# A feed-forward kernel on one core: the first butterfly of x moved from GpSimd into PSUM accumulation, early and late turns moved from DMA to TensorE, and all engine programs written out anew

## The reference

```python
w = weights[conditions]
y = jnp.einsum('bct,bcd->bdt', x, w)          # tokens (b, d), 512 features
h = hbitlinear(y, w_up, 8)                    # w_up (1024, 512)
h = jnp.square(jax.nn.relu(h))
out = x + hbitlinear(h, w_down, 8)            # w_down (512, 1024)

def hbitlinear(x, w, bits):
    xq = act_quant(fwht(x), bits)             # Walsh-Hadamard, then absmax quantization per token
    wq = weight_quant(w)                      # ternary, one scale: mean |w|
    return jnp.einsum('bsd,fd->bsf', xq, wq)
```

## Time and profile before

| what | us |
|---|---|
| median of 3 runs | 282.44 |
| lowest, highest run | 282.28, 285.0 |
| span of the profiled execution | 279.9 |
| what lies around the span (median less span) | 2.5 |
| PE busy | 246.1 (88%) |
| DVE busy | 204.7 (73%) |
| POOL busy | 181.4 (65%) |
| ACT busy | 147.4 (53%) |

### The profile page before, as it was taken

The page is one execution under the profiler, slowest core; times in us unless marked ns, Lnnn a source line. Parts: engine busy times, 40 slices in busy tenths (PEclk is TensorE's granted clock), DMA queues, the critical chain, the costliest instruction groups (busy, mean ns, idle before and its releaser), DMA issues.

```text
span 279.9 us, 6739 instructions
## 1 busy us (share of the span) xinstructions
PE 246.1 (88%) x2116; PEld 203.6 (73%) x2116; DVE 204.7 (73%) x341; ACT 147.4 (53%) x193; POOL 181.4 (65%) x231
## 2 busy tenths in 40 slices
PE   0266899799999999999999999999999899985872
PEld 0266797797979797979797888888888687754441
DVE  0145557799888697888878796969697977887632
ACT  2143588765647465655656565556462766641220
POOL 1333133869797979697979788887976467278510
PEclk9999999999999999999999999999999999998899
DMA  6865963245563745585664437434443325553364
GB/s 188 305 210 204 191 158 51 42 122 95 143 107 92 154 122 89 143 143 128 155 191 87 122 75 215 94 94 98 116 84 106 81 57 109 135 112 75 75 86 141
DMA packets 67369, 34.96 MB, mean 125 GB/s; under 512 B 57490, under 2 KB 57618, under 8 KB 67346
## 3 DMA queue, kind: packets, MB, share of 16 engines
q10 hardware_dynamic: 52432, 14.75, 28.4%
q1 hardware_dynamic: 14914, 19.93, 23.3%
HBM read 13.70 MB, written 8.39 MB: 79 GB/s over the span
## 4 chain that ended last, share of the span: by engine, by line
PE 61%; issue 9%; DMA 8%; POOL 6%; DVE 5%; ACTq 4%; ACT 3%; SPq 2%; POOLq 0%; DVEq 0%
PE u_ps L750 15%; PE h_ps L737 14%; PE o_ps L761 13%; PE y_ps L708 10%; PE z_ps L721 8%; DMA zqT<-zq 4%; POOL p L422 4%; ACTq L527 2%; DMA uqT<-uq 2%; ACT uq L547 2%; POOL u_deq L430 1%; DVE u_max L931 1%; ACTq L554 1%; DVE y L893 1%; DMA w_pair<-in_L_cond_weights_dram 1%
## 5 line engine op out<-in xcount | busy, mean ns | idle before, releaser
L422 POOL TENSOR_TENSOR p<-g 128x512 f32<-128x512 f32 x64 | 80.9, 1287 | 23.6 <-DVE g L924 22.9
L750 PEld LDWEIGHTS u_ps<-had_sb,p 128*128 128x128 f32 x512 | 61.0, 193 | 12.2 <-POOL p L422 7.1
L750 PE MATMUL u_ps<-had_sb,p 128*128 128x128 f32 x512 | 63.8, 278 | 6.8 <-POOL p L422 4.4
L737 PE MATMUL h_ps<-zqT,w_upT 128*128 128x256 f16 x512 | 61.8, 272 | 2.5 <-ACT g L534 1.3
L761 PE MATMUL o_ps<-w_downT,uqT 128*128 128x512 f16 x256 | 61.7, 384 | 2.4 <-DMA uqT<-uq 2.4
L385 POOL TENSOR_TENSOR x_half<-x_all 128x512 f32<-128x512 f32 (+1 forms) x32 | 40.9, 1300 | 25.9 <-PE y_ps L708 15.3
L737 PEld LDWEIGHTS h_ps<-zqT,w_upT 128*128 128x128 f16 x512 | 49.4, 98 | 9.5 <-issue 2.0
L547 ACT ACTIVATE uq<-u_ps,u_mul 128x1024 f16<-128x1024 f32 x32 | 35.6, 1114 | 34.2 <-DVE u_mul L944 28.2
L534 ACT ACTIVATE g<-h_ps 128x512 f32<-128x512 f32 x64 | 37.7, 595 | 21.8 <-PE h_ps L737 10.1
L931 DVE TENSOR_REDUCE u_max<-u_ps 128x1 f32<-128x1024 f32 x32 | 39.0, 1218 | 10.8 <-PE u_ps L750 10.7
L708 PE MATMUL y_ps<-w_pair,x_half 64*128 64x64 f32 x512 | 35.4, 293 | 12.1 <-DMA w_pair<-in_L_cond_weights_dram 12.1
(11 more groups left out here) (35 smaller groups left out, 142.1 us busy)
## 6 DMA issues: line engine op xcount, KB each, us to landing
x_all<-in_x_dram SPq DMA_DIRECT2D x32, 256.0 KB, 3.3
out_dram<-out_sb SPq DMA_DIRECT2D x32, 256.0 KB, 2.3
w_raw<-in_L_ffn_w_up_dram ACTq DMA_DIRECT2D x4, 512.0 KB, 4.4
w_raw<-in_L_ffn_w_down_dram SPq DMA_DIRECT2D x4, 512.0 KB, 4.9
w_pair<-in_L_cond_weights_dram SPq DMA_DIRECT2D x64, 16.0 KB, 2.2
zqT<-zq ACTq DMA_TRANSPOSE x32, 2.7
uqT<-uq ACTq DMA_TRANSPOSE x32, 3.1
had_sb<-in_hadamard_dram ACTq DMA_DIRECT2D x1, 64.0 KB, 3.6
```

Source lines behind the costliest of these rows:

```text
L422: nc.gpsimd.tensor_tensor(new[:, :, m, :], old[:, :, 0, :], old[:, :, 1, :], (ALU.add, ALU.subtract)[m]).then_inc(s_p8[k], 1)
L737: mm = nc.tensor.matmul(h_ps[u % 2][:, i, :], w_upT[:, q, f * P:(f + 1) * P], zqT[par][:, q, :], start=(q == 0), stop=(q == TC - 1))
L750: mm = nc.tensor.matmul(u_ps[:, c * P:(c + 1) * P], p8[par][:, c, k * P:(k + 1) * P], had_sb[:, :], start=True, stop=True)
```

## The change

`x_outer` is gone. `project` now streams for the first half of x's features the two copies (w, w), 128 columns, and for the second half (w, minus w), accumulated in the same PSUM place; ACT writes minus w once per tile (`negate_w`). Both kernels issue 16 matmuls per tile here. The two z halves of a tile are turned by one DMA, except tile 0, which PE turns (`first_turn`, with a copy by DVE). The last tile's u is turned by PE as well (`last_turn`, `last_copy`). The second half of tile 0's z goes into an h bank; the second halves of u in tiles 14 and 15 go into the h banks, and the second halves of their output into `z_ps`. Scale columns have a place per tile, so that the copies `keep_z` and `z_now` fall away. PE begins with 24 matmuls on constants (`warm`). x has 8 buffers of a tile instead of 16 tiles in place, w has 8 instead of 4, out_sb has two sets, zqT five. All five programs are written out call by call, without a loop, and in a new order.

```diff
-            def x_outer(t, half, par, h):
...
-                nc.gpsimd.tensor_tensor(x_half[h][:, :, :], xt[:, :, 0, :], xt[:, :, 1, :],
-                                        (ALU.add, ALU.subtract)[h]).then_inc(s_xh[h], 1)
+            def negate_w(t):
+                act.wait_ge(s_wc[t % NW], 16 * BT * (t // NW + 1))
+                nc.scalar.activation(ws[t % NW][:, :, 1, :], ws[t % NW][:, :, 0, :], ACT.Copy, scale=-1.0)\
+                    .then_inc(s_ws, 1)
...
-                                nc.tensor.matmul(y_ps[:, b, l, h, j, :],
-                                                 x_half[h][rows, j, l * P:(l + 1) * P], w[rows, j, :],
-                                                 start=True, stop=True)
+            for l in range(2):
+                for j in range(KP):
+                    for h in range(2):
+                        for b in range(2):
+                            w = ws[t % NW][rows, j, 0:1, :].broadcast_to([C, 2, C]) if h == 0 \
+                                else ws[t % NW][rows, j, :, :]
+                            mm = nc.tensor.matmul(y_ps[:, b, l, :, j, :],
+                                                  xs[t % NX][rows, j, h * 256 + l * P:h * 256 + (l + 1) * P], w,
+                                                  start=(h == 0), stop=(h == 1))
...
+            def warm():
+                for i in range(WARM):                              # WARM = 24
+                    nc.tensor.matmul(o_ps[:, 0:P], ones[:, :], ones[:, :], start=True, stop=True)
+            def first_turn(k):
+                for q in range(TC):
+                    mm = nc.tensor.transpose(zT_ps[:, (k * TC + q) * P:(k * TC + q + 1) * P],
+                                             zq[0][:, k, q * P:(q + 1) * P], ident[:, :])
+            def last_turn(k):
+                for m in range(FC):
+                    mm = nc.tensor.transpose(uT_ps[k][:, m * P:(m + 1) * P], uq[(TILES - 1) % 2][:, k, m * P:(m + 1) * P],
+                                             ident[:, :])
+        def own_home(t, k):
+            return k == 1 and t in LAST                            # tiles 14 and 15
+        def z_home(t, k):
+            return h_flat[:, T:2 * T] if (t, k) == (0, 1) else z_ps[:, :]
+        def u_home(t, k):
+            return h_flat if own_home(t, k) else u_ps[:, :]
+        def o_home(t, k):
+            return z_ps[:, :] if own_home(t, k) else o_ps[:, :]
...
+                act.dma_start(zqT[t % NZT][:, :, :, :].rearrange("p k q n -> p (k q) n"),
+                             zq[t % 2][:, :, :].rearrange("p k t -> p (k t)"), transpose=True)\
```

More of the change, by code:

```diff
@@ L196, in after @@
         def after(eng, semaphore, count):
[L198 to L231, removed]
+            if count > 0:
+                eng.wait_ge(semaphore, count)
@@ new lines, in _ @@
+            up(2, 3)
+            up(2, 2)
+            had_u(0, 1)
+            up(3, 1)
+            had_z(4, 1)
+            up(3, 0)
+            down(0, 0)
+            had_u(1, 0)
+            project(6)
+            had_z(5, 0)
+            up(3, 3)
+            up(3, 2)
+            down(0, 1)
+            had_u(1, 1)
+            up(4, 1)
+            had_z(5, 1)
+            up(4, 0)
+            project(7)
+            had_u(2, 0)
+            had_z(6, 0)
+            up(4, 3)
+            up(4, 2)
@@ new lines, in _ @@
+            down(1, 0)
+            had_u(2, 1)
+            up(5, 0)
+            had_z(6, 1)
+            down(1, 1)
+            had_u(3, 0)
+            up(5, 1)
+            project(8)
+            had_z(7, 0)
+            up(5, 2)
+            up(5, 3)
+            down(2, 0)
+            had_u(3, 1)
+            up(6, 1)
+            had_z(7, 1)
+            down(2, 1)
+            project(9)
+            had_u(4, 0)
+            had_z(8, 0)
+            up(6, 0)
+            up(6, 3)
+            down(3, 0)
@@ new lines, in _ @@
+            up(6, 2)
+            had_u(4, 1)
+            had_z(8, 1)
+            up(7, 1)
+            down(3, 1)
+            up(7, 0)
+            had_u(5, 0)
+            had_z(9, 0)
+            project(10)
+            up(7, 2)
+            up(7, 3)
+            had_u(5, 1)
+            had_z(9, 1)
+            down(4, 0)
+            up(8, 0)
+            up(8, 1)
+            had_u(6, 0)
+            had_z(10, 0)
+            down(4, 1)
+            up(8, 2)
+            project(11)
+            had_u(6, 1)
@@ new lines, in _ @@
+            up(8, 3)
+            had_z(10, 1)
+            down(5, 0)
+            project(12)
+            had_u(7, 0)
+            had_z(11, 0)
+            up(9, 0)
+            up(9, 1)
+            down(5, 1)
+            up(9, 2)
+            had_u(7, 1)
+            up(9, 3)
+            had_z(11, 1)
+            down(6, 0)
+            up(10, 0)
+            had_u(8, 0)
+            up(10, 1)
+            had_z(12, 0)
+            project(13)
+            up(10, 2)
+            had_u(8, 1)
@@ new lines, in _ @@
+            up(10, 3)
+            had_z(12, 1)
+            down(6, 1)
+            up(11, 0)
+            had_u(9, 0)
+            up(11, 1)
+            down(7, 0)
+            had_z(13, 0)
+            project(14)
+            up(11, 2)
+            had_u(9, 1)
+            up(11, 3)
+            down(7, 1)
+            had_z(13, 1)
+            up(12, 0)
+            had_u(10, 0)
+            down(8, 0)
+            up(12, 1)
+            up(12, 2)
+            had_z(14, 0)
+            up(12, 3)
@@ L851, in _ @@
+            down(15, 0)
+            down(15, 1)
         @block.vector
```

1843 lines of the change are left out of this document (1138 added, 705 removed).

## The result

| | us |
|---|---|
| before, median of 4 runs | 283.72 (282.28 to 285.23) |
| changed, median of 4 runs | 271.28 (269.82 to 272.7) |
| ratio, 95% interval | 0.9596 (0.953 to 0.9661) |
| span of the profiled execution (272.7 us) | 270.9 |
| predicted | 268.0, range 259 to 279 |

What follows compares the result with a forecast made beforehand. The prediction took PE to bound the middle at 14.3 us per tile, with time lost at both ends. Work of 234.0 us plus losses of 31.5 gave span 265.5, and 2.5 outside it made 268.0 us, range 259 to 279.

Steps and rivals of the forecast that it cites:

- The sum: Whole kernel: 234.0 us of PE work plus 31.5 lost make span 265.5; with 2.5 outside the span, 268.0.
- the ramp: Start of the kernel, before PE becomes continuous: PE loses 20 us (15 to 25) instead of 28.5, 8.5 gained.
- the middle: Stretch between the two ends: PE loses 3 us (1 to 9) instead of 1.1 under the order written by hand.
- the end: Last tiles: PE loses 8.5 us (6 to 13) instead of 17.9, 9.4 gained.
- What bounds the kernel: Kernel before: PE alone bounds the middle at 14.3 us per tile; 28.5 us are lost ahead of it, 17.9 after.
- project: PE's project matmuls: the doubled columns hide under the weight load, adding 0.02 us per tile, 0.3 us in all.
- Hidden under PE: ACT in each tile: negate_w, below 0.4 us per instruction, raises ACT's work from 8.3 to 8.7 us without delaying PE.
- Work taken from POOL: Removing x_outer from POOL: worth nothing in the middle, about 2.6 us of latency ahead of the first project.
- Rival 1: project on PE: the added columns are not hidden, 3.55 us instead of 1.93 each, 294 us in all; 6 in 100.
- Rival 2: Middle: DVE or ACT takes PE's place as the bound, waits of 0.8 us per tile, 276 to 280 us; 22 in 100.
- Rival 3: Ramp: it does not shorten because w_up loaded early delays x and w in the DMA queues, about 275 us; 12 in 100.
- Rival 4: Both ends do better: losses of 15 us in the ramp, 1 in the middle, 6.5 at the end, 259 us; 10 in 100.

Runs made afterwards that it cites:

- experiments 2: The changed kernel with project streaming 64 columns per matmul instead of 128, the butterfly between the halves left out of the computation: one execution, 270.83 us.
- experiment 3: The changed kernel with project's loops turned, all matmuls of the first batch and then all of the second: one execution, 294.14 us.
- experiment 1: The changed kernel with negate_w of tiles 8 to 15 moved later on ACT's list: 263.95 us, ratio to the kernel before 0.9331.
- experiment 6: experiment 1's kernel with 11 x buffers, early x loads, x's butterfly back on GpSimd, 64-column project, no negate_w: 275.19 us; 263.5 with only the buffers and loads.
- experiment 10: experiment 1's kernel with tile 0's z turned by one DMA from ACT's queue instead of by PE: 269.73 us, ratio to the kernel before 0.9583.
- experiment 7: experiment 1's kernel without the 24 matmuls on constants at PE's beginning: 263.72 us, ratio to the kernel before 0.9338.
- experiment 8: experiment 1's kernel with all u in u_ps and all outputs in o_ps, also in tiles 14 and 15: 274.44 us, ratio to the kernel before 0.9837.
- experiment 9: experiment 1's kernel with the last tile's u turned by two DMAs from ACT's queue instead of by PE: 263.74 us, ratio to the kernel before 0.9361.
- the repaired order: experiment 1's kernel with 11 x buffers, early x loads and y_split of tile 0 ahead of the first weight_abs: 262.58 us, ratio to before 0.931.

## Why the prediction was right, and where it was off

**The sum.** The measured time lies in the range, but the terms do not all hold. Against the forecast the ramp lost 0.2 us less, the middle 8.9 more, the end 2.4 less, and the work was 0.9 less: 5.4 us more on the span. That the end and the work paid back 3.3 of the middle's 8.9 is luck. At the median 3.3 us are left, as 1.8 us lie around the profiled span, not 2.5, and that execution is 1.4 us above the median.

**What bounds the kernel; the two ends.** Right in size. PE runs at 14.3 us a tile wherever it runs, and the gain came from the ends: 19.8 lost in the ramp for 20 forecast, 6.1 at the end for 8.5.

**project.** Right in mechanism: experiments 2 and 3 show that the columns cost next to nothing and that this hangs on the pair running together. One reading behind it was wrong. The two records of `weight_sum` do not start 108 ns apart but 31 (at 36.030 and 36.061 us; the second is the longer one, 253 ns). What lies 110 and 111 ns apart is the start of their weight loads and the next one, on PEld (35.923, 36.033, 36.144), while 4 columns are streamed. So the conclusion stands, on other records: the load sets this pace. The size was 0.06 us per tile, not 0.02: 1.0 us instead of 0.3.

**"Hidden under PE".** This is the step that failed most. The prediction priced `negate_w` as 16 ACT instructions of under 0.4 us (0.31 measured) and 8.7 us of ACT work per tile, and put it under PE. It did not ask what the instruction waits for and who is queued behind it. `negate_w` ties ACT's strict list to SP's gathers, and the new list asks for tile 14's at 88 us, before SP has issued them. One wait of 4.76 us, with the clock behind it, cost 7.3 us (experiment 1) and makes up 7.0 of the 8.9 by which the middle's loss exceeded its 3. The prediction had SP's time per gather, 1.3 us, in hand for the ramp, but did not carry it through 62 of them.

**"Work taken from POOL is worth nothing in the middle".** Not so in the new order, by experiment 6: putting it back costs 11.7 us, and in the profiled execution half of the loss lies in the middle. POOL's spare time was the wrong measure. What counted was how long `g_last`, and ACT's `relu` and `quant_u` behind it, stand in the queue, and that instructions of DVE and POOL lengthen each other where they meet. In the order before they seldom met: 6 of DVE's 64 butterflies overlap with one on POOL (`g_inner` 1254 ns in the page before, 1214 after). How the 11.7 divide between slower work, a later ramp and my placing of `x_outer` stays open; another placing was not tried.

**The ramp.** The sum was right by luck, the path less so. The first `project` started at 10.90 and not 9.7 (its gathers), `y_split` stood behind `weight_abs`, and the second `project` ran at 3.65 us with the granted clock at 0.60 to 0.54, so that the weight scale came at 23.1, not 19.2. For the way from the scale to the first `had_u` the prediction kept the 28.1 us of the kernel before; it took 24.7. The two errors cancel: `had_u` at 47.8 where 19.2 + 28.1 gives 47.3, and the first `quant_u` at 52.3 where 51 to 53 was forecast. Why that stretch is shorter was not taken apart; the turn of tile 0 on PE is a candidate, since without it the first `had_u` comes 7.0 us later (experiment 10). The early clock was not worth its term (experiment 7).

**The end.** The sizes hold: PE waits 0.94 us for the residual ahead of `down` (12, 1), as forecast, and 0.36 for `quant_u`. In the new order the second homes are needed for all of it (12.3 us without them, experiment 8) and the last turn for nothing (experiment 9). But the waits that come back without the homes are for `quant_u` and residuals, not those of before for `g_last` (3.15 and 1.27) and a turning DMA (1.50); what took these away, the new order or POOL's lighter list, no run shows.

**Rivals.** Rival 1 was false here and real in experiment 3. Rival 2, a wait in the middle, came true in size (8.9 us more than my 3), but by ACT waiting for SP's gathers, which the prediction names nowhere. Rival 3 did not occur. Rival 4 came true at the end (6.1 for its 6.5) and nowhere else: even the repaired order, with 262.58, stays above its 259.

## What to carry to other kernels

When work is moved to another engine, list what the new instruction waits for and what stands behind it in that engine's list, before its duration: here an instruction of 0.31 us cost 7.3. A queue that issues many small transfers has a rate of its own (1.24 to 1.29 us each here, against 16 KB of data); multiply it out over the whole kernel and compare with when each consumer's list asks for them. And the parts of a tuned order do not add up: taken out one at a time, with the order left as it was tuned for all of them, they cost 11.7, 10.5, 5.8 and 3.8 us, together 32, more than the 20 us that the repaired kernel gains in all.

## What was not expected of the hardware

- Doubling the streamed columns of 64-row fp32 matmuls is nearly free (1.93 to 1.99 us for 32 records, pairs 112 ns apart with either) if neighbours use different row halves, and the same matmuls take 3.50 in the other order.
- Butterflies on GpSimd and VectorE lengthen each other where they meet (VectorE's from 1.22 to as much as 2.37 us). How often they meet is a matter of order more than of load: 6 of 64 in the kernel before with GpSimd busy 181.4 us, 27 of 64 in experiment 6 with 180.3.
- After 4.17 us of idle PE the granted clock was 0.50 and the next `had_u` took 3.78 us against 1.95 to 2.05, so that the hole cost 7.0. After 2.14 us (experiment 6, at 117 us) it was the same, and 5.0 were lost; after 3.54 us in the ramp of experiment 1 the clock stayed up.
- 24 matmuls on constants brought the first `project` of 128 columns with the batches in turn to 2.06 us instead of 3.79 in every profiled execution, kept the second one fast in only some, and changed nothing in the end.
